# Expert units: pass 1 on two heads at once, from copies of their own in two 64-row halves

## The reference, cut to what matters

```python
_, top2 = jax.lax.top_k(probs, 2)
for e in range(e_total):
    member = (top2 == e).any(-1)
    w_tok = jnp.where(member, probs[..., e], 0.0)
    order = jnp.argsort((~member).astype(jnp.int32), axis=-1, stable=True)
    xg = jnp.take_along_axis(x, order[..., None], axis=1)
    validg = jnp.take_along_axis(member, order, axis=1)
    q, k, v = xg @ wq[e] + bq[e], xg @ wk[e] + bk[e], xg @ wv[e] + bv[e]      # 16 heads of 16
    att = jnp.einsum('bqhd,bkhd->bhqk', q, k) * sm_scale
    att = jnp.where(validg[:, None, None, :], att, -1000000000.0)
    y = jnp.einsum('bhqk,bkhd->bqhd', jax.nn.softmax(att, axis=-1), v)
    out = out.at[bidx, order].add(wg[..., None] * (y @ wo[e] + bo[e]))
```

## Time and profile before

| | |
|---|---|
| median of 3 runs | 4015.29 us (4011.35 to 4018.01) |
| the profiled execution | 4016.7 us |
| its span, first to last instruction | 4015.0 us |
| PE busy | 3419.1 us (85%) |
| DVE busy | 2376.0 us (59%) |
| ACT busy | 2093.3 us (52%) |
| granted TensorE clock, mean | 0.93 of full speed |
| first unit ends at | 1024.45 us |
| 14 middle units | 1024.45 to 2693.98 us |

### The profile page before, as it was taken

The page is one execution under the profiler, slowest core; times in us unless marked ns, Lnnn a source line. Parts: engine busy times, 40 slices in busy tenths (PEclk is TensorE's granted clock), DMA queues, the critical chain, the costliest instruction groups (busy, mean ns, idle before and its releaser), DMA issues.

```text
span 4015.0 us, 56809 instructions
## 1 busy us (share of the span) xinstructions
PE 3419.1 (85%) x21573; PEld 1655.3 (41%) x21574; DVE 2376.0 (59%) x3496; ACT 2093.3 (52%) x4546; POOL 987.9 (25%) x845
## 2 busy tenths in 40 slices
PE   6999999878899999998999888663799888888895
PEld 3444445333334333334434334332344344435674
DVE  5565655656575757565675544323767878785423
ACT  2666665535576666666675554331365455562221
POOL 1241522322202020202101122222324241200474
PEclk7999999979999999999999998876799999998897
DMA  6454536323313030404213234333433232304588
GB/s 184 152 162 123 155 106 197 83 80 87 90 26 94 22 94 22 99 17 100 70 36 83 62 86 112 96 94 102 115 87 109 78 110 61 85 14 132 131 200 227
DMA packets 307098, 399.90 MB, mean 100 GB/s; under 512 B 33677, under 2 KB 271931, under 8 KB 299893
## 3 DMA queue, kind: packets, MB, share of 16 engines
q1 hardware_dynamic: 275718, 341.63, 30.9%
q0 software_dynamic: 26880, 50.49, 5.4%
q10 hardware_dynamic: 4224, 4.19, 0.3%
HBM read 230.48 MB, written 156.17 MB: 96 GB/s over the span
## 4 chain that ended last, share of the span: by engine, by line
PE 62%; DVE 19%; DMA 8%; issue 4%; ACT 3%; POOL 2%; SPq 2%; ACTq 0%; another core or an unknown queue 0%; DVEq 0%; POOLq 0%
PE PSUM L855 15%; PE PSUM L815 12%; DVE M L1084 12%; PE PSUM L833 11%; PE PSUM L746 6%; DMA KS<-mk_d 3%; PE PSUM L877 3%; PE PSUM L792 3%; PE PSUM L654 2%; DVE best L1453 1%; PE PSUM L863 1%; DVE XR L1456 1%; PE PSUM L818 1%; ACT P L1021 1%; PE PSUM L836 1%
## 5 line engine op out<-in xcount | busy, mean ns | idle before, releaser
L1084 DVE TENSOR_REDUCE M<-PSUM 128x1 f32<-128x896 f32 (+7 forms) x1702 | 1703.0, 1032 | 999.8 <-PE PSUM L815 569.4
L1021 ACT ACTIVATE P<-PSUM 128x512 f32<-128x512 f32 (+2 forms) x3520 | 1581.0, 502 | 771.3 <-PE PSUM L833 501.3
L815 PE MATMUL PSUM<-KS,QS 99*128 99x512 bf16 (+3 forms) x3592 | 939.3, 344 | 261.2 <-DVE M L1084 86.9
L833 PE MATMUL PSUM<-QS,KS 101*128 101x512 bf16 (+2 forms) x3520 | 1066.8, 341 | 51.0 <-DMA QS<-MR 17.1
L855 PE MATMUL PSUM<-P,VA 128*17 128x384 f32 (+3 forms) x7040 | 768.8, 514 | 0.0
L833 PEld LDWEIGHTS PSUM<-QS,KS 101*128 101x128 bf16 x3520 | 331.0, 99 | 771.0 <-ACT P L1021 391.9
L815 PEld LDWEIGHTS PSUM<-KS,QS 99*128 99x128 bf16 x3592 | 317.4, 100 | 674.8 <-DVE M L1084 289.9
L706 POOL TENSOR_TENSOR QF<-QF,PH 128x1024 f32<-128x1024 f32 (+4 forms) x94 | 154.5, 1644 | 671.5 <-ACT PH L986 631.0
L746 PE MATMUL PSUM<-XT,W 128*128 128x512 f32 (+2 forms) x656 | 297.8, 581 | 8.6 <-DMA bq<-in_L_ffn_bk 7.0
L618 POOL DMA_DIRECT2D QS<-MR x63 | 35.9, 570 | 903.9 <-ACT MR L1013 903.9
L855 PEld LDWEIGHTS PSUM<-P,VA 128*17 128x17 f32 x7040 | 136.0, 96 | 229.6 <-issue 196.5
(11 more groups left out here) (213 smaller groups left out, 3150.7 us busy)
## 6 DMA issues: line engine op xcount, KB each, us to landing
qk_d<-PH SPq DMA_DIRECT2D x120, 256.0 KB
xg_d<-GX SPq DMA_DIRECT2D x19, 1152.0 KB, 12.7
yg_d<-GX SPq DMA_DIRECT2D x17, 1152.0 KB, 7.9
XF<-xg_d SPq DMA_DIRECT2D x17, 1024.0 KB, 7.2
VA<-n_L_ffn_expert_gate_up_w SPq DMA_DIRECT2D x64, 256.0 KB, 3.7
QS<-qk_d SPq DMA_DIRECT2D x36, 384.0 KB, 6.3
KS<-qk_d SPq DMA_DIRECT2D x36, 384.0 KB, 6.1
qk_d<-PH SPq DMA_DIRECT2D x48, 224.0 KB
```

The lines of the kernel that those rows point to most:

```text
L815: mm = e.matmul(slot_heads(s, hb)[:, x, a:b], QS[0:KA, g, h + x, 128 * qt:128 * qt + 128], KS[0:KA, g, h + x, a:b], start=True, stop=not d ...
L833: mm = e.matmul(s[:, 0:q1 - q0], KS[0:KB, g, j, 128 * kt:128 * kt + 128], QS[0:KB, g, j, q0:q1], start=True, stop=not diag, skip_group_che ...
L1021: e.activation(P[:, m % NP, 0:q1 - q0], s[:, 0:q1 - q0], ACT.Exp, scale=ly.scale).then_inc(S["act_p"], 1)
L1084: e.tensor_reduce(m[:, qt, h:h + hb], v[:, :, 0:kn], AX.X, ALU.max).then_inc(S["dve_a"], 1)
```

## The change

In middle units (`Order.paired`), both for the unit itself and for group 0 of the next, pass 1 reads other tiles and contracts other rows.

- **Copies.** `Q1` (two buffers in `COS` and `SIN`) and `K1` (two buffers in the half of `VA` that units don't use) hold for one group two duos of heads: head 2d in rows 0 to 48, head 2d + 1 in rows 64 to 112. The 49 rows are three part products (hi hi, mid hi, hi mid; the other three are left out of the maximum) and the mask. Pass 2 still uses `QS` and `KS`.
- **Loads.** Task `qa` (i, w, g) loads them from `qk_d`: four DMAs for each of Q and K and each group, 32 in a unit, and a fifth for the mask with K of i = 2. `on1` writes the ones once, in the first unit. `vo` writes the ones of `VA` again in the final unit.
- **Matmuls.** A slot now takes, for nt > 4, two heads and one chunk of up to 512 keys (four slots a query tile: k = 0, 1 are chunk 0, k = 2, 3 chunk 1), for nt 3 and 4 two heads, for less four. Head 2d goes to bank 0 and head 2d + 1 to bank 1, as two matmuls of 64 x 128 tiles of the array, the first in rows 0 to 63, the second in rows 64 to 127. Slots, matmuls and elements that DVE reduces stay the same in number (at nt 7: 112 slots, 224 matmuls a unit).
- **Reduction.** DVE writes two heads' maxima at once, those of chunk 1 to `MX`; for nt > 4 `mh` has one more instruction, the maximum of `M` and `MX`.
- **Plan.** `step` is 0.72 nt² in middle units, and `s1` tasks are spread evenly.

```diff
+    def duos(self):
+        return [0] if self.nt <= 2 else list(range(2 * self.nch))
...
+        self.paired = layer.name == "moe" and not layer.first and not layer.final
...
+    def halves(self, i):
+        return 2 if self.paired and self.layer.of(i).nch == 2 else 1
+    def pair_loads(self, i, wi, g):
+        return f"ahead_pair{wi}" if (i, g) == (2, 1) else f"pair{wi}{g % 2}"
+    def last_score(self, i, g):
+        ly = self.layer.of(i)
+        return "s1", i, g, ly.nt - 1, ly.duos()[-1] if self.paired else 4 - ly.heads(ly.nt - 1)
...
+    if paired:
+        tiles = [(qt, k) for qt in range(layer.nt) for k in layer.duos()]
+        cost = [1.0] * len(tiles)
...
-    step, small = max(0.84 * nt * nt, 3.4), nt <= 4
+    step, small = max((0.84 if layer.first or layer.final else 0.72) * nt * nt, 3.4), nt <= 4
...
+    done = [0.0] + [first[g][0] + 0.82 * first[g][1] for g in range(1, 4)]
+    if paired:
+        ev += [(-1.2 + 0.1 * w, ("qa", 1, w, 2)) for w in range(2)]
+        ev += [(done[1] + 0.3 + 0.1 * w, ("qa", 1, w, 3)) for w in range(2)]
...
+                if paired:
+                    ev += [(max(done[2], back) + 0.1 + 0.1 * w, ("qa", 2, w, 0)) for w in range(2)]
+                ev += [(max(done[3], back, 52.0 * layer.first) + 0.5 + 0.1 * w, ("qa", 2, w, 1)) for w in range(2)]
...
+        Q1 = [x[:, :].bitcast(BF16).rearrange("p (x n) -> p x n", x=2) for x in (COS, SIN)]
+        K1 = VF[:, 0:2048].bitcast(BF16).rearrange("p (b x n) -> p b x n", b=2, x=2)
...
+                elif kind == "s1" and O.paired:                                   # PE
+                    _, _, g, qt, k = task
+                    for wi in range(2):
+                        if (i, g) == (1, 1):
+                            w.carried(f"ahead_pair{wi}", 64 + 16 * wi)
+                        else:
+                            w.wait_ge(f"pair{wi}{g % 2}", "qa", i, wi, g)
+                    c, m = k // 2, ly.wide(k // 2)
+                    for x, duo in enumerate((0, 1) if ly.nt <= 2 else (k % 2,)):
+                        for half in range(2):
+                            r = slice(64 * half, 64 * half + 49)
+                            mm = e.matmul(s[:, half, m * x:m * x + m], Q1[g % 2][r, duo, 128 * qt:128 * qt + 128],
+                                          K1[r, g % 2, duo, 512 * c:512 * c + m], start=True, stop=True)
+                    mm.then_inc(S["pe_a"], 1)
...
+                    top = (MX if k >= 2 else M)[:, g % 2, qt, :]                  # DVE, s1
...
+                        e.tensor_reduce(top[:, 2 * (k % 2):2 * (k % 2) + 2], s[:, :, 0:m],
+                                        AX.X, ALU.max).then_inc(S["dve_a"], 1)
...
+                    if O.halves(i) == 2:                                          # DVE, mh
+                        e.tensor_tensor(M[:, g % 2, 0:ly.nt, :], M[:, g % 2, 0:ly.nt, :], MX[:, g % 2, 0:ly.nt, :],
+                                        ALU.max).then_inc(S["dve_x"], 1)
+                        e.wait_ge(S["dve_x"], O.at("dve_x", *task) - 1)
...
+                elif kind == "qa":                                                # SP
+                    _, _, wi, g = task
+                    b = g % 2
+                    if i == 1:
+                        w.carried(f"ahead_st{wi}", 48)
+                    else:
+                        w.wait_ge(f"qst{wi}0", "qs", i, wi, 0)
+                    if (i, g) == (1, 3):
+                        w.wait_ge("pe_a", *O.last_score(1, 1))
+                    elif i == 2 and O.paired:
+                        w.wait_ge("pe_a", *O.last_score(1, 2 + g))
...
+                    for half in range(2):
+                        for r, m0, m1 in ((0, 0, 2), (32, 0, 1)) if wi == 0 else ((0, 1, 3), (32, 2, 3)):
+                            part = slice(64 * half + r, 64 * half + r + 16 * (m1 - m0))
+                            e.dma_start(Q1[b][part, :, 0:n] if wi == 0 else K1[part, b, :, 0:n],
+                                        qk_d[wi][m0:m1, :, 4 * g + half:4 * g + 4:2, 0:n].rearrange(
+                                            "m d h n -> (m d) h n")).then_inc(done, 16)
```

More of the change, by code:

```diff
@@ L36 @@
             + [f"mrow{g}" for g in range(4)]
+            + ["pair_ones"] + [f"pair{w}{b}" for w in range(2) for b in range(2)]
             + ["sh_rows", "sh_weights", "first_weights"] + [f"sh_res{b}" for b in range(B)])
@@ L164, in raises @@
         return {"s2": [("pe_s", 1), ("act_p", 1)], "pv": [("pe_v", 1)], "po": [("act_o", 1)],
[2 rows of a table removed]
+                "mh": [("dve_x", self.halves(ix[0]))] if kind == "mh" else None, "ml": [("dve_x", 1)], "bs": [("dve_x", 1)], "ba": [("dve_x", 1)], "rs": [("dve_x", 1)],
+                "on": [], "on1": [("pair_ones", 32)], "vo": [("dve_x", 1)],
+                "qa": [(self.pair_loads(*ix), 64 + 16 * (ix[0] == 2 and ix[1] == 1))] if kind == "qa" else None, "kd": [], "cs": [("dve_x", 1)], "ca": [("dve_x", 1)], "cr": [("dve_x", 1)],
                 "x2": [("dve_x", 2)], "rc": [("dve_x", 1)], "rx": [("act_x", 1)],
@@ L280, with first_pass @@
 SHARED = shared_pieces(range(B))
-def first_pass(layer, i, g, t0, long):
+def first_pass(layer, i, g, t0, long, paired=False):
     ev = []
@@ L297, in first_pass, with attention_steps @@
     return ev
-def attention_steps(layer, i, first, second):
+def attention_steps(layer, i, first, second, paired=False):
     ev = []
@@ L469, in unit_order @@
     over = [t + 1.06 * step for t, _ in second]
-    ev += attention_steps(layer, 1, first, second)
+    paired = not (layer.first or layer.final)
+    ev += attention_steps(layer, 1, first, second, paired)
+    done = [0.0] + [first[g][0] + 0.82 * first[g][1] for g in range(1, 4)]
+    if paired:
+        ev += [(-1.2 + 0.1 * w, ("qa", 1, w, 2)) for w in range(2)]
+        ev += [(done[1] + 0.3 + 0.1 * w, ("qa", 1, w, 3)) for w in range(2)]
+    if layer.first:
+        ev.append((50.0, ("on1", 2)))
+    if layer.final:
+        ev.append((0.02, ("vo", 1)))
     ev += [(-1.0 + 0.1 * w + 0.05 * g, ("ql", 1, w, 2 + g)) for w in range(2) for g in range(2)]
@@ L997, in attention_act @@
                     w.wait_ge("pe_v", "pv", i - 2, 3, ly.nch - 1, ly.nt - 1)
+                    if O.final and i == 2:
+                        w.carried("ahead_pair0", 64)
+                        w.carried("ahead_pair1", 80)
                     w.wait_ge("pe_a", *task)
@@ L1122, in attention_dve @@
                         [128, 2, 128])).then_inc(S["dve_x"], 1)
+                elif kind == "vo":
+                    w.carried("ahead_pair0", 64)
+                    w.carried("ahead_pair1", 80)
+                    e.memset(VA[:, 0, :, :, 16:17], 1.0).then_inc(S["dve_x"], 1)
                 elif kind == "bb":
@@ L1581, in attention_sp @@
                     w.wait_ge(*O.split(i, wi, g2))
+                    if O.paired and g2 == 0:
+                        w.carried(f"ahead_pair{wi}", 64 + 16 * wi)
+                    elif O.paired:
+                        for g in (2, 3):
+                            w.wait_ge(f"pair{wi}{g % 2}", "qa", 1, wi, g)
                     for g in (2 * g2, 2 * g2 + 1):
@@ L1611, in attention_sp @@
                             done, 16)
+                elif kind == "on1":
+                    w.wait_ge("unit_masks", "bm", 0)
+                    for x in range(2):
+                        e.dma_start(Q1[x][48:113:64, :, :].rearrange("p x n -> p (x n)"),
+                                    d["c_rows"][0:2, 0:2 * T]).then_inc(S["pair_ones"], 16)
+                elif kind == "qa":
[3 more added lines that the diff above has]
+                        w.carried(f"ahead_st{wi}", 48)
+                    else:
+                        w.wait_ge(f"qst{wi}0", "qs", i, wi, 0)
[3 more added lines that the diff above has]
+                        w.wait_ge("pe_a", *O.last_score(1, 2 + g))
+                    if i == 2:
+                        w.wait_ge("unit_masks", "bm", 0)
+                    done = S[O.pair_loads(i, wi, g)]
+                    if (i, g) == (2, 1):
+                        e.sem_clear(done)
+                    for half in range(2):
[4 more added lines that the diff above has]
+                                            "m d h n -> (m d) h n")).then_inc(done, 16)
+                    if i == 2 and wi == 1:
+                        masks = mk_d[row(v["nu"]), 0:n].rearrange("o (h n) -> o h n", h=1)
+                        if O.layer.first:
+                            rows, times = K1[48:113:64, :, :, 0:n].rearrange("p b x n -> p (b x) n"), 4
+                        else:
+                            rows, times = K1[48:113:64, b, :, 0:n], 2
+                        e.dma_start(rows, masks.to_broadcast([2, times, n])).then_inc(done, 16)
                 elif kind == "mr" and not moe:
```

19 lines of the change are left out of this document (14 added, 5 removed), and 2 rows, old and new, of the table ONE_BANK.

## The result

The changed kernel takes 4002.34 us (median of 19 runs, 3991.15 to 4016.73), the kernel before, on the same chip, 4014.73 us (19 runs, 4003.66 to 4023.12). The ratio over all runs is 0.9973, 95% interval 0.9964 to 0.9983 (that of the two medians is 0.9969): 0.27% faster, where 1.1% was forecast. The direction was right and the time lies in the range, but three quarters of the gain are missing.

The account below looks back on a forecast made before the run. PE and DVE share the bound. Unit savings of 4 x 5.5 + 3 x 3.7 + 4 x 1.2 + 3 x 2.7 make 46 us, less 1 for first and final units: 45, forecast 3970 us, range 3905 to 4040.

Parts of the forecast that it names:

- What bounds the kernel: Middle units: PE is short where most time goes; PE and DVE share the bound, cycle by cycle.
- Streams: Pass 1 slots on PE: halves overlap fully, 21.3 us less PE time a unit at nt 7, 15.6 at nt 6.
- Changes of shape: PE, between row halves and other tiles: 0.093 us each, 18.6 us for 200 more at nt 7, 15.3 at nt 6.
- The long cycles: Three-slot cycles between `pv`s: 0.27 us less each, 17 in a unit of nt 7, 4.6 us.
- The plan: Order of tasks in middle units: no term; long stretches of one pass together were named as a sign of error.
- DVE and the extra maximum: DVE reduces as many elements; one new maximum per group, 0.2 us with a wait, costs 0.6 us a unit at nt 7.
- DMAs: SP's queue: 32 more issues a unit, 15 us of SP, costed at nothing at nt 7 and 6.
- nt 2: PE's mask wait before pass 1 of group 2 shrinks to 1 to 2 us; 2.7 us less a unit, three units.
- free changes: Rival on PE: changes of shape cost nothing for row halves, then DVE binds; 106 us less, 3909; chance 0.14.
- a change costs more than 0.123: Slower rival on PE: row-half changes cost more than column ones; 4040 at 0.14 us each, up to 4115; chance 0.21.
- the partial overlap: Pass 1 halves on PE overlap only in part: 30% of the streams' saving lost, 46 us; within a rival of 0.15.
- Nothing comes of it: Rival: halves overlap in part or long cycles become DVE's alone; time as before, 4015 us; chance 0.15.

Follow-up runs that it names:

- experiment 2: Kernel before, with middle-unit pass 1 matmuls taking half of each slot's keys and the reduction reading those twice: 3953.36 us, ratio 0.9810.
- experiment 5: Changed kernel with step 0.84, pass 1 slots moved beside `pv` at nt 6 and 7: 4001.28 us, ratio 0.9966; `pv` moved instead: 3987.12 us, 0.9930.
- experiment 4: Kernel before, with the mask copy of groups 2 and 3 issued ahead of the `ql` loads: 4011.24 us, ratio 0.9990.

## Why the forecast was off, step by step

Units of a size added up in the profiled runs, in us (before is one profiled run; the middle columns are means of two and three, and at nt 2 the two of the changed kernel are 5 us apart):

| | before | changed | changed, old step | forecast of the difference |
|---|---|---|---|---|
| 4 of nt 7 | 788.6 | 784.4 | 778.5 | -22 |
| 3 of nt 6 | 472.8 | 473.7 | 472.8 | -11 |
| 4 of nt 3 | 250.6 | 254.8 | 242.0 | -5 |
| 3 of nt 2 | 157.6 | 143.4 | 143.5 | -8 |

- **What bounds the kernel:** right. PE and DVE share the bound cycle by cycle; taking 20.9 us of streams off PE alone (experiment 2) gives 11.4. ACT, which the forecast left out, binds in places too, as the waits there and in experiment 5 show.
- **Streams, -21.3 and -15.6 (15.8 by its own factors):** measured 20.9 and 15.4. The full overlap of the halves, for which no row of before existed, is there.
- **Changes of shape, +18.6 for 200 at 0.093:** measured 20.2 with the old step (303 changes) and 21.1 with the new one (310), at 0.10 each. This is the step that failed inside the mechanism, by its size: the term was 1.6 us a unit too small at nt 7, and with it the streams' net gain shrinks from 2.7 to 0.7. At nt 6 the 168 changes more cost about 17 us for 15.3, and the net of 0.3 becomes a loss. By the Trainium skill, TensorEngine Tiling (Array Packing), Key Properties, a change of mode drains TensorE; the trace agrees in that every change costs, 0.10 us in both directions, for row halves as for columns.
- **The long cycles, -4.6:** somewhat too large. Of the 5.5 us a unit that the forecast had at nt 7, 2.7 were the net of the streams, so 2.8 were left for shorter waits (with the maximum's 0.6 taken off); PE's waits fell by 2.0 (20.5 to 18.5). At nt 6, where 3.4 were left for them, they fell by about 3 (19.0 to 20.0 before, 16.4 with the old step). Why they fell by less wasn't taken apart further. With the small gaps (0.8) it is 3.5 us a unit of nt 7 with the old step, for 5.5.
- **The plan, priced at nothing:** the main failure. The forecast listed "if the new plan put long stretches of one pass together" as something that would make it wrong, but no term and no rival had a number for the new step. It costs 21 us: by the table 6 at nt 7 and 13 at nt 3, where it takes all that the change gave. With the old step nt 3 gained 8.6 us where 5 were forecast: PE's waits for a bias, 2.4, 2.3 and 1.5 before, which the forecast took to stay, are 0 to 1.0 there, and gone with the new step, which brings others in their place.
- **The granted clock, priced at nothing:** the kernels with row halves spend 10 to 34 us more at 1.2 GHz in the first seven middle units than the kernel before. At nt 6 this eats what the terms give: by the same split as in the table, a unit with 1.5 us for the low clock takes 154.5 us, one with 3.7 takes 156.7 (both with the old step), and one with 9.5 takes 159.1 (the changed kernel). What brings these stretches no run tried, and the rows of before gave no price for them.
- **DVE and the extra maximum:** 0.7 us more of DVE at nt 7 (126.67 for 125.94), as costed; PE's waits for the turned maxima grew by 0.2 to 0.4 us (1.8 to 2.0 and 2.2), for 0.6.
- **DMAs:** 26 MB more in SP's queue cost nothing that shows at nt 7; PE's wait for SP at a unit's start is 1.7 us in both. At nt 2 they show as the 1.15 and 1.31 us of experiment 4.
- **nt 2, -8:** measured -14. The wait of 4.85 is gone altogether, where 1 to 2 us were expected to stay; what the mask alone gives is left open (experiment 4).
- **The rivals:** free changes is out, with 0.10 at each (its sum also had a slip: 2.72 and 3.42 less 5.43 is 0.7, where it took 0.6). That a change costs more than 0.123 is out, and so is the partial overlap: the two halves take 0.39 us together, as one matmul does. The ratio of the Trainium skill, TensorE: Matmul & The Clock Gate, Part 3, taken there as an estimate, would have lost 30% of the streams' saving; the trace shows none lost. "Nothing comes of it" came nearest in time, by a cause that it didn't name.

Put together: 45 us were forecast. The new step takes 21 of them. With the old step the three ratios give 26, 33 and 25 us. By the table nt 7 and 6 then fall short of the forecast by 23 us, and nt 3 and 2 give 10 more than it. Of the 23 the price of changes is about 2 us in each of these seven units; the lower clock and the waits are what remains, not separated by a run of their own.
